# Returning the experts' results by a scatter inside the expert loop, with GpSimd adding the early batches' rows

## The reference

```python
shared = silu(x @ shared_w_gate.T) * (x @ shared_w_up.T) @ shared_w_down.T   # 704 wide
shared = shared * sigmoid(x @ shared_gate_w.T)
probs = softmax(x @ gate_w.T)                      # 16 experts
rw, sel = top_k(probs, 2); rw = rw / rw.sum()      # two choices per token
g, h = halves of x @ w_gate_up[e]; out_e = (silu(g) * h) @ w_down[e]
out = sum over the two chosen experts of rw * out_e + shared
```

## Time and profile before

| what | value |
|---|---|
| three runs, device time | 773.67, 771.24, 773.57 us (median 773.57) |
| profiled execution: its span | 768.6 us |
| its own time | not listed apart from the three runs; the median lies 5.0 us above the span |
| busy: TensorE, VectorE, ScalarE, GpSimd | 91%, 68%, 52%, 43% of the span |
| HBM traffic | 86.66 MB read, 76.02 MB written |

### The profile page before, as it was taken

How to read it: one execution, slowest core, us unless ns; L and a number is a source line. 1 busy time by engine, 2 the same in 40 slices (tenths; PEclk the granted TensorE clock), 3 DMA queues, 4 the chain that set the end, 5 groups by cost and what they waited for, 6 DMA issues and landing times. The chain is left out here.

```text
span 768.6 us, 16584 instructions
## 1 busy us (share of the span) xinstructions
PE 698.2 (91%) x5906; PEld 555.8 (72%) x5906; DVE 523.6 (68%) x1158; ACT 400.9 (52%) x779; POOL 330.9 (43%) x678
## 2 busy tenths in 40 slices
PE   3589999999999999999999687999899999899992
PEld 3456576676767667676656586888699999798882
DVE  4387788887888888787853678456655555438874
ACT  3126667566675757757666415334556666512330
POOL 5205445273552725525283327777300000067774
PEclk9789999999999999999999979999899999999997
DMA  4958577576875758847433297656446556378764
GB/s 131 320 202 305 195 273 244 208 247 243 302 262 188 257 205 302 276 169 241 153 112 108 85 387 239 213 188 209 158 139 190 187 186 193 112 231 266 255 222 134
DMA packets 100398, 164.02 MB, mean 213 GB/s; under 512 B 7648, under 2 KB 74208, under 8 KB 96096
## 3 DMA queue, kind: packets, MB, share of 16 engines
q1 hardware_dynamic: 94176, 146.18, 56.3%
q0 software_dynamic: 6144, 16.79, 6.6%
HBM read 86.66 MB, written 76.02 MB: 212 GB/s over the span
## 5 line engine op out<-in xcount | busy, mean ns | idle before, releaser
L685 DVE TENSOR_REDUCE neg_max<-ps_w 128x1 f32<-128x512 f32 (+3 forms) x352 | 202.7, 633 | 43.7 <-PE ps_w L790 43.5
L604 ACT ACTIVATE probs<-ps_w 128x512 f32<-128x512 f32 x320 | 165.3, 617 | 10.1 <-PE ps_w L806 10.0
L435 POOL TENSOR_TENSOR pool_scratch<-minus_half 1x1 f32<-1x1 f32 x190 | 34.8, 183 | 232.2 <-ACT probs L604 199.4
L1202 POOL DMA_INDIRECT ex<-yg_dram,slots x64 | 64.9, 1014 | 150.2 <-DMA yg_dram<-y 131.0
L467 POOL TENSOR_SCALAR_AFFINE_SELECT probs<-probs 128x256 f32<-128x256 f32 (+1 forms) x224 | 93.8, 430 | 0.0
L1190 POOL DMA_INDIRECT xg_dram<-srow,slots x64 | 70.7, 1104 | 32.7 <-issue 19.2
L1233 ACT ACTIVATE rows_held<-ps_f 128x512 f32<-128x512 f32 (+1 forms) x42 | 25.0, 596 | 110.4 <-PE ps_f L190 110.4
L817 PE MATMUL ps_w<-probs,v_aug 128*32 128x512 f32 (+3 forms) x1024 | 77.2, 443 | 0.3 <-DVE logits_all L713 0.3
L188 PE MATMUL ps_f<-stacks 128*128 128x512 f32 x154 | 61.6, 400 | 4.1 <-DVE rows_held L1433 4.1
L817 PEld LDWEIGHTS ps_w<-probs,v_aug 128*32 128x32 f32 x1024 | 31.2, 111 | 41.1 <-issue 32.7
L190 PE MATMUL ps_f<-stacks 128*128 128x512 f32 x154 | 60.5, 393 | 0.0
(11 more groups left out here) (187 smaller groups left out, 1768.0 us busy)
## 6 DMA issues: line engine op xcount, KB each, us to landing
qk_dram<-projected SPq DMA_DIRECT2D x96, 256.0 KB, 6.2
stacks<-qk_dram SPq DMA_DIRECT2D x16, 1024.0 KB, 7.4
heads_held<-qk_dram SPq DMA_DIRECT2D x12, 1024.0 KB, 6.4
xg_dram<-zeros SPq DMA_DIRECT2D x20, 512.0 KB, 10.6
srow<-xg_dram SPq DMA_DIRECT2D x40, 256.0 KB, 2.9
ex<-experts SPq DMA_DIRECT2D x4, 1536.0 KB, 14.8
yg_dram<-projected SPq DMA_DIRECT2D x20, 256.0 KB, 2.2
yg_dram<-y SPq DMA_DIRECT2D x20, 256.0 KB, 2.2
```

The source lines that it names most:

```text
L435: ticks = Ticks(pool, pool_ticks, lambda: pool.tensor_tensor(out=pool_scratch[:, 0:1], in0=minus_half[0:1, 0:1], in1=minus_half[0:1, 0:1], ...
L604: act.activation(probs[:, g, p * PAIR + half * BANK:p * PAIR + (half + 1) * BANK], ps_w[:, plan.bank(kind, which, half), :], ACT.Exp).then ...
L685: dve.tensor_reduce(out=neg_max[u][:, qt, first:first + len(heads)], in_=bank[:, 0:len(heads) * width].rearrange("p (h n) -> p h n", h=len ...
L1202: pool.indirect_dma_start(out=back[:, m, c, :], out_offset=None, in_=yg_rows, in_offset=bass.IndirectOffsetOnAxis(ap=slots[:, c, m:m + 1], ...
```

## The change

The results are no longer stored by slot and gathered by token. Each row of `xg_dram` gets two more numbers, its token's number and the slot of its second choice (`ROW` = 258), written by GpSimd into the rows before their scatter. In the expert loop VectorE works out from them, for each slot of a pair, a row of `y2_dram` (`place_of`: token, or token + 4096 for a second choice; an empty slot gets a row behind these), and GpSimd scatters the two result tiles there. Behind the loop SP loads a batch's rows with two plain transfers (`load_back`). `FIRST` becomes 5. For batches 0 to 4 GpSimd multiplies the rows by their weights and adds them to the sums loaded from `y1_dram`; VectorE adds those of batches 5 to 7 (`add_own`) into `x1_of[b]`, which for these batches is loaded from `x1_dram` and goes to the output without a stop in `y1_dram`. SP's order behind the loop is written anew. The zeroing of `xg_dram` writes the larger number 2^20 and -1 into the two new columns.

```diff
-FIRST = 4
+FIRST = 5
 PARITY = B // 2
-EXPERTS_FROM = [0, 0, 4, 8, 12, 16]
+EXPERTS_FROM = [0, 0, 4, 8, 12, 16, 16, 16]
 LOADS = 4
 PER_LOAD = E // LOADS
-TILES_BESIDE = {4: (0, 0, 0, 0, 0, 0, 1), 5: (1, 1, 1, 2, 1, 1, 2), 6: (1, 1, 2, 1, 1, 2, 1), 7: (1, 1, 2, 1, 2, 1, 1)}
-assert sum(sum(v) for v in TILES_BESIDE.values()) == NT - TB
-
-
-SCATTERED_BESIDE = {0: (), 1: (2, 3, 4), 2: (5, 6), 3: (7,)}
-
-
-def tiles_beside(b, j):
-
-    counts = [n for batch in range(FIRST, B) for n in TILES_BESIDE[batch]]
-    first = sum(counts[:7 * (b - FIRST) + j])
-    return range(first, first + TILES_BESIDE[b][j])
+OWN_BESIDE = {FIRST + 1: (1, 1, 1, 1, 1, 1, 2)}
+OWN_BESIDE.update({b: (0, 1, 1, 1, 1, 0, 0) for b in range(FIRST + 2, B)})
+assert sum(sum(v) for v in OWN_BESIDE.values()) == (B - FIRST) * TB
+ROW = D + 2
+TOKENS = B * S
+EMPTY = float(2 ** 20)
+
+
+SCATTERED_BESIDE = {0: (), 1: (2, 3), 2: (4, 5), 3: (6, 7), 4: (), 5: ()}
...
+    slot_numbers = iota_t
+    place = projected[:, 2 * EW + 2 * TB * D + E + MOE_TILES + 2 * NT:][:, 0:MOE_TILES].bitcast(mybir.dt.int32)
-    loaded = spent[:, 2 * NT * D:2 * NT * D + (B - 1) * TB * D].rearrange("p (b t d) -> p b t d", b=B - 1, t=TB)
+    loaded = spent[:, 2 * NT * D:2 * NT * D + FIRST * TB * D].rearrange("p (b t d) -> p b t d", b=FIRST, t=TB)
+    x1_of = [x1 if b < FIRST else (x1, y1[:, :, :])[(b - FIRST) % 2] for b in range(B)]
+    back_v = y2_dram[0:2 * TOKENS].rearrange("(c b t p) d -> b c p t d", c=2, b=B, p=P)
...
+                sp.wait_ge(m_place, q - (FOUR - 1))
             sp.dma_start(xg[:, q % FOUR], xg_pairs[q]).then_inc(moe_in[q % FOUR], 16)
-
-        def store_pair(q):
-            sp.wait_ge(m_y, q + 1)
-            sp.dma_start(yg_pairs[q], y_e[q % FOUR]).then_inc(moe_out[q % FOUR], 16)
 
         def slot(n):
             if is_pair(n + 1 + FOUR):
                 load_pair(n + 1 + FOUR)
-            if is_pair(n - 1):
-                store_pair(n - 1)
 
         def tiles():
             for par in range(2):
@@ -1128,35 +1138,60 @@
             load_xn(FIRST + 1)
             slots_of_loop(slot)
             for n in range(FOUR):
-                sp.wait_ge(moe_out[n], 4 * TILE_PAIRS)
-
-        def load_y1(b):
-            sp.wait_ge(x1_left, 16 * (b + 1))
-            sp.dma_start(loaded[:, b], item(y1_v, b)).then_inc(y1_in[b], 16)
+                sp.wait_ge(moe_out[n], 8 * TILE_PAIRS)
+            sp.wait_ge(m_xT, TILE_PAIRS)
...
+        def load_own(b):
+            if b >= FIRST + 2:
+                sp.wait_ge(own_out, 16 * (b - 1 - FIRST))
+            sp.dma_start(x1_of[b], x1_v[b]).then_inc(own_in[b % 2], 16)
+
+        def load_back(b):
+            for c in range(2):
+                sp.dma_start(back[:, b * TB:(b + 1) * TB, c, :], back_v[b, c]).then_inc(back_in[b], 16)
+
+        def load_old(b):
+            if b >= FIRST:
+                return
+            sp.dma_start(loaded[:, b], y1_v[b]).then_inc(y1_in[b], 16)
+            load_back(b)
+
+        def store_old(b):
+            if b >= FIRST:
+                return
+            sp.wait_ge(old_both, b + 1)
+            sp.dma_start(out_v[b], loaded[:, b]).then_inc(result_out, 16)
 
         def second_half(b, more):
-            load_x1(b)
             if b == FIRST:
-                load_y1(0)
-                load_y1(1)
-            else:
-                load_y1(b - 1)
+                load_own(FIRST)
+                load_back(FIRST)
+                load_old(0)
+                load_own(FIRST + 1)
+                load_back(FIRST + 1)
+                load_old(1)
+                return
             load_next_xn(b)
-            for j in range(FT + 1):
-                for m in tiles_beside(b, j):
-                    old, t = divmod(m, TB)
-                    if t == TB - 1:
-                        sp.wait_ge(both_added, m + 1)
-                        sp.dma_start(item(out_v, old), sums_of[old % 2]).then_inc(result_out[old % 2], 16)
-                        if old + 2 < FIRST:
-                            load_y1(old + 2)
-            if more:
+            if b == FIRST + 1:
+                sp.wait_ge(both_added, TB)
+                sp.dma_start(out_v[FIRST], x1_of[FIRST]).then_inc(own_out, 16)
+                load_own(FIRST + 2)
+                load_back(FIRST + 2)
+            for old in range(2 * (b - FIRST), 2 * (b - FIRST) + 2):
+                load_old(old)
+                store_old(old - 2)
+            if b < B - 1:
                 sp.wait_ge(y_done, TB * (b + 1))
-                sp.dma_start(item(y1_v, b), x1[:, :, :]).then_inc(x1_left, 16)
-            else:
-                for first in range(0, TB, 2):
-                    sp.wait_ge(y_done, TB * b + first + 2)
-                    sp.dma_start(item(out_v, b)[:, first:first + 2], x1[:, first:first + 2, :]).then_inc(x1_left, 16)
+                sp.dma_start(out_v[b], x1_of[b]).then_inc(own_out, 16)
+                if b + 2 < B:
+                    load_own(b + 2)
+                    load_back(b + 2)
+                return
+            for old in range(2 * (b - FIRST), FIRST):
+                store_old(old)
+            for first in range(0, TB, 2):
+                sp.wait_ge(y_done, TB * b + first + 2)
+                sp.dma_start(out_v[b][:, first:first + 2], x1_of[b][:, first:first + 2]).then_inc(own_out, 16)
...
+                if b >= 2:
+                    pool.wait_ge(scattered[b % 2], SCATTERS * (b // 2))
+                pool.iota(srow[:, b % 2, :, D], pattern=[[P, TB]], base=b * S, channel_multiplier=1, allow_small_or_imprecise_dtypes=True).then_inc(ids_made, 1)
+                pool.tensor_copy(srow[:, b % 2, :, D + 1], slot_f[:, 1, b * TB:(b + 1) * TB]).then_inc(ids_made, 1)
+                pool.wait_ge(ids_made, 2 * (b + 1))
             for c in range(2):
                 pool.indirect_dma_start(out=xg_rows, out_offset=bass.IndirectOffsetOnAxis(ap=slots[:, c, n:n + 1], axis=0),
                                         in_=srow[:, b % 2, t, :], in_offset=None).then_inc(scattered[b % 2], 16)
-        for par in range(2):
-            pool.wait_ge(scattered[par], SCATTERS * PARITY)
-        for n in range(FOUR):
-            pool.wait_ge(moe_out[n], 4 * TILE_PAIRS)
-        pool.wait_ge(m_xT, TILE_PAIRS)
-
-        for m in range(NT):
-            if m >= TB:
-                pool.wait_ge(gathered[m % TB], 32 * (m // TB))
+        pool.wait_ge(routed, 1)
+        pool.iota(slot_numbers[:, :], pattern=[[P, MOE_TILES]], base=0, channel_multiplier=1, allow_small_or_imprecise_dtypes=True).then_inc(slot_numbers_made, 1)
+
+        for q in range(TILE_PAIRS):
+            pool.wait_ge(m_place, q + 1)
+            pool.wait_ge(m_y, q + 1)
+            for t in range(2):
+                pool.indirect_dma_start(out=y2_dram, out_offset=bass.IndirectOffsetOnAxis(ap=place[:, 2 * q + t:2 * q + t + 1], axis=0),
+                                        in_=y_e[q % FOUR][:, t, :], in_offset=None).then_inc(moe_out[q % FOUR], 16)
+
+        for b in range(FIRST):
+            ms = slice(b * TB, (b + 1) * TB)
+            pool.wait_ge(back_in[b], 32)
             for c in range(2):
-                pool.indirect_dma_start(out=back[:, m, c, :], out_offset=None, in_=yg_rows,
-                                        in_offset=bass.IndirectOffsetOnAxis(ap=slots[:, c, m:m + 1], axis=0)).then_inc(gathered[m % TB], 16)
+                for m in range(b * TB, (b + 1) * TB):
+                    pool.tensor_scalar(out=back[:, m, c, :], in0=back[:, m, c, :], scalar1=weight[:, c, m:m + 1], scalar2=None, op0=ALU.mult)                        .then_inc(old_scaled, 1)
+            pool.wait_ge(old_scaled, 2 * TB * b + TB)
+            pool.wait_ge(y1_in[b], 16)
+            pool.tensor_tensor(out=loaded[:, b], in0=loaded[:, b], in1=back[:, ms, 0, :], op=ALU.add).then_inc(old_first, 1)
+            pool.wait_ge(old_scaled, 2 * TB * (b + 1))
+            pool.wait_ge(old_first, b + 1)
+            pool.tensor_tensor(out=loaded[:, b], in0=loaded[:, b], in1=back[:, ms, 1, :], op=ALU.add).then_inc(old_both, 1)
...
-                act.wait_ge(moe_out[q % FOUR], 16 * (q // FOUR))
+                act.wait_ge(moe_out[q % FOUR], 32 * (q // FOUR))
...
-            dve.wait_ge(x1_in, 16 * (b + 1))
+            if b < FIRST:
+                dve.wait_ge(x1_in, 16 * (b + 1))
+            else:
+                dve.wait_ge(own_in[b % 2], 16 * ((b - FIRST) // 2 + 1))
+            if b > FIRST:
+                dve.wait_ge(both_added, TB * (b + 1 - FIRST))
...
-            total = sums_of[b % 2 if b < B - 1 else 2][:, t, :]
-            dve.scalar_tensor_tensor(out=total, in0=back[:, m, c, :], scalar=weight[:, c, bass.ds(m, 1)],
-                                     in1=total if c or b == B - 1 else loaded[:, b, t, :], op0=ALU.mult, op1=ALU.add).then_inc(done, 1)
-
-        def add_first(m):
-            dve.wait_ge(gathered[m % TB], 32 * (m // TB + 1))
```

(30 more changed lines are left out.)

70 lines of the change are left out of this document (33 added, 37 removed).

## The result

| | device time, us | ratio to before |
|---|---|---|
| before, measured beside it | 773.62 (771.24 to 773.73, 4 runs) | |
| after | 790.04 (789.18 to 790.77, 4 runs) | 1.0239, 95% interval 1.0215 to 1.0263 |

By the medians the change costs 16.4 us; the forecast said 9.4, a ratio of 1.012, which lies far outside the interval.

A forecast was written before the change was run, and what follows sets the result against it. Gathers bound the old kernel's end; now GpSimd's adds would: from 712.0, 17.6 + 13.3 to 742.9, then 26.4 and half of 8.0 to 773.3, stores to 778.0, plus 5.0: 783.0 us, 1.2% slower; range 769 to 791.

The forecast's parts named there:

- the three operations: Expert loop: three dependent tiny VectorE operations per pair, 0.211 us each, about 0.70 with gaps; counted as costing nothing.
- the forecast's mechanism: Behind the loop: GpSimd's adds for five batches, slowed by VectorE, end at 773.3 and close the span at 778.0.
- the forecast's sign: End of the kernel: GpSimd's sums end some 15 to 20 us after TensorE's last matmul.
- the product: GpSimd behind the loop: each one-input 128x256 product takes 0.48 us, 8 per batch, 3.8 us.
- exclusion: Behind the loop: VectorE's two-input work keeps GpSimd out for whole operations, 13.3 us in batch 6, half of batch 7's 8.0.
- Behind it: After GpSimd's end: batch 4's store and the halves behind it take 0.1, 3.1 and 1.5 us to 778.0.
- Around the span: Outside the profiled span: 5.0 us between span and device time, added to each end worked out.
- VectorE loses time too: Behind the loop: VectorE loses at most one GpSimd operation per meeting, covered by 20 us of adds handed over.
- Rival 1: Behind the loop: TensorE sets the end, GpSimd done by about 753; 762.9 us, chance 0.13.
- The fourth own tile: VectorE behind the loop: its fourth own tile comes at 723.0; SP waits for it before loading batch 2's rows.
- Rival 2: Behind the loop: GpSimd sets the end without exclusion, waiting for batch 2's rows; 774.8 us, chance 0.22.
- Rival 3: Expert loop: scatters or tiny operations slow it by 0.2 us for each of 40 pairs, 8 us; 791, chance 0.07.

The follow-up runs named there:

- e2: The changed kernel with GpSimd's products and sums for batches 0 to 4 left out, all transfers kept: 759.92 us, ratio 0.985.
- e1: The changed kernel with a second operator, times 1.0, in GpSimd's products: 780.63 us, ratio 1.0116.
- e7: The changed kernel with GpSimd's one-operator products taking a constant, 0.5, in place of the column of weights: 787.09 us, one run.
- e10: The changed kernel with GpSimd's two sums per batch left out and its products kept: 770.4 us, one run.
- e12: Four batches ahead with VectorE making all adds, plus a tiny GpSimd fill at the very end: 765.96 us, 4.3 more than without the fill.
- e3: The changed kernel with ScalarE making the early batches' products and GpSimd only the sums: 777.21 us, ratio 1.0061.
- e8: The changed kernel with two-operator products, all early rows asked for behind the first burst and next input rows asked for earlier: 775.21 us, ratio 1.0047.
- e4: The changed kernel with four batches ahead of the loop instead of five, all else as changed: 767.18 us, ratio 0.9954.
- e5: The changed kernel with four batches ahead, two-operator products, and early rows and next input rows asked for earlier: 768.11 us, ratio 0.9948.

## Why the prediction was right in direction and wrong in size

**Right.** The loop took the scatters and the tiny operations at no cost: 2.80 us per pair, the three operations 0.15 to 0.16 us each where I had taken 0.21. Its last result came at 696.3 (695.5 forecast). GpSimd started at 713.4 (712.0), a sum took 2.34 (2.37), and SP's queue held the stores in the order described. That GpSimd, not TensorE, sets the end is the forecast's mechanism, and e2 confirms it: without GpSimd's part the time falls by 30 us. GpSimd ended 22 us behind TensorE's last matmul, where the forecast's sign was 15 to 20.

**The step that failed: the product.** "The product lies between a select of the same shape, 0.397, and a two-operator scaling, 0.544; I take 0.48, the middle." It takes 0.90 to 0.92. The two-operator scaling was no upper end, since the one-operator form is the slower one (e1, e7). Per batch that is 7.2 us in place of 3.8, over five batches 17 us (16 for the whole batches, since the sums and GpSimd's own waits came out 1 us less). Had I priced it so, and left all else, the forecast would have been 800.

**The term that hid it: exclusion.** I charged GpSimd 17.3 us for VectorE's two-input work; it was 8.1. "If one keeps the other out for whole operations" holds for sums, not for products: products and VectorE share, each somewhat slower (e10). The first two batches ended at 742.4, 0.5 from my 742.9, and only because the errors cancel there: a start 1.4 later, 6.4 more for the batches, 8.3 less for exclusion. That is luck. A right sum in the middle is no proof of its terms.

**The account.** GpSimd's end: forecast 773.3; start +1.4, five batches 60.0 in place of 44.0, so +16.0, exclusion -9.2: 781.5, as measured. Behind it 7.5 us to the span's end in place of 4.7, +2.8: I had counted the stores, which would have closed the span at 786.4 (the last data at 785.6, and 0.8), and not the DRAIN that follows GpSimd's last instruction (e12). Around the span 1.0 in place of 5.0, -4.0: the runs since then list 1.6 to 1.8 us between an execution and its own span, so the profiled execution of before was itself quicker than its median, by some 3 us. 783.0 + 1.4 + 16.0 - 9.2 + 2.8 - 4.0 = 790.0.

**What was counted at nothing and wasn't.** "VectorE loses time too ... and has that in hand before TensorE waits for it" was wrong. It lost 4.1 us at one meeting (two adds in 5.14 us in place of 1.0), and TensorE waited 4.1 us behind the loop. In the changed kernel GpSimd's end hides that; once GpSimd is quicker it comes out level with it (e3, e8), and with four ahead it sets the end (e4).

**The rivals.** Rival 1 needed batch 2's rows before 727; they came at 742.5 (forecast 738.7). The transfers are not the cause: the store landed in 3.0 us in place of 4.1, and the burst took 11.4 in place of 11.6. The fourth own tile came at 728.0 in place of 723.0, because GpSimd's sums held VectorE up; in e2 it came at 723.4. Rival 2, no exclusion, was right for the products (each engine slower, neither shut out) and wrong for the sums, and it had the same wrong price. Rival 3's loop didn't slow.

**The Trainium skill's rule** ("SBUF — State Buffer", section "Who interferes with whom": whole-instruction exclusion between a two-input VectorE operation and a GpSimd instruction that reads SBUF). For the sums the runs agree: 0.68 us became 2.80, ending half a microsecond after the sum. For the one-operator products they don't: 0.482 became 0.586.

**Open.** Why the one-operator form is the slower one, and what GpSimd does in the 7.3 us of its DRAIN: the runs show sizes only. Nor why the DRAIN ends 6.0 us behind the last gather of the kernel before. It is not shown either why the first scattered rows came later in some executions (e5, e12).

## What to carry to other kernels

Price an operation on GpSimd by the row of its very form, and distrust a bound taken from a form with more arithmetic: the one with two operators was twice as fast. Work given to GpSimd beside VectorE isn't free for the engine behind VectorE: sums of two SBUF operands hold VectorE's two-input operations up for their whole length, that delays TensorE and even the loads that wait for VectorE, and TensorE's clock fell to a half behind the longer waits, while the same adds on VectorE took a third of the time and cost nothing where it had room. Ask how long the stretch is in which moved work must fit: here 60 us of work had 46 us from its first data to TensorE's end (and should have been done some 3.5 us before even that: the span of e2 ends 4.0 us after its last matmul, and 7.5 us follow GpSimd's last instruction), and one batch less was worth some 22 us.

## What the runs showed of the hardware

- The span ends 7.5 us after GpSimd's last instruction if nothing else ends later: 7.49 to 7.56 in seven kernels, and 7.5 behind a fill of 0.11 us (e12). A DRAIN on GpSimd's queue takes 7.3 of them. In the kernel before it ended 6.0 us behind the last gather, 2.2 ahead of the end.
- GpSimd's scaling of 128x256 float32 takes 0.92 us with one operator and a column scalar, 0.85 with a constant, and 0.46 with a second operator that multiplies by 1.0 (the last with VectorE nearly idle).
- Two VectorE adds beside two GpSimd sums of 128x1024 take 5.17 us in place of 1.00; VectorE's operation with an input in PSUM (L1481) kept its 0.69 beside the same sums.
- GpSimd's one-input products and VectorE's two-input operations run side by side: 1.18 us for a product in place of 0.90, and 0.10 us more for an add.
- TensorE's granted clock fell from 1.00 to 0.50 (2.4 to 1.2 GHz) for some 7 us each in e1 (732.8 to 739.8, waits of 2.3 and 2.3 us), e8 (733.7 to 740.5, waits of 2.3 and 2.7) and e4 (733.8 to 740.7, a wait of 2.2). With the changed kernel's waits of 1.5, 0.8 and 1.8 us it stayed at 1.00.
